# Macaron transformer layer on eight cores: the q/k/v projections of the next head group move into the query blocks of the current one

## The chip, the cores and the metric

The program runs on all eight cores of one Trainium2 chip. Each core computes one of the eight sequences of the batch, with no exchange between cores. The metric is the time of one execution on the slowest core, in microseconds (us). The cores' engines are TensorE (PE, matmuls), VectorE (DVE), ScalarE (ACT), GpSimd (POOL) and SyncE (SP); each works through its own list of instructions in order and waits on semaphores for the others.

## What is computed

The input is 2048 tokens of width 1024 per core. The layer is a mixture-of-experts feed-forward step, an attention step, and the same feed-forward step again, each on a layer-normed input and added to the running x. The change is in the attention alone:

```python
proj = x @ w_in                        # x: layer-normed [2048, 1024]
k, v, q = jnp.split(proj, 3, axis=-1)  # 16 heads of 64 each
scores = jnp.einsum('bhqd,bhkd->bhqk', q, k) * scale
scores = scores + _tisa_bias(amplitudes, sharpness, offsets, s)[None]
weights = jax.nn.softmax(scores, axis=-1)
attn = jnp.einsum('bhqk,bhkd->bhqd', weights, v)
gated = attn.transpose(0, 2, 1, 3).reshape(b, s, d) @ w_gate + b_gate
a, g = jnp.split(gated, 2, axis=-1)
return a * jax.nn.sigmoid(g)
```

The bias depends only on head and on the distance between query and key, so the kernel keeps exp(bias) as a table of 4095 values per head in DRAM (`etab_d`) and multiplies exp(scores) by it.

## The kernel before

Everything is written with explicit semaphores. `ph.op(engine, ...)` appends an instruction to one engine's list, `ph.wait(engine, event)` makes the next instruction of that list wait. So the order in which the Python loops run is the order of each engine.

`attn_phase` (from L723) works on `NGRP` = 8 groups of two heads. One group g of the loop has these parts:

- **flush_pending** finishes the last query block of the group before. `flush_a` (L816): TensorE turns the row of softmax sums with four small transposes (L824), VectorE takes the reciprocal (L832), GpSimd stores it to DRAM (`rbc_scr`) and, when the store has landed, reads it back spread over the partitions (`at_bca`). `flush_b` (L848): VectorE waits for that read and multiplies the block's result by it (L858 into `at_af` for the even head, L870 into `at_stag` for the odd one, from which GpSimd moves it on by DMA).
- **Projection** (L906): for k, v, q in turn and for four chunks of 512 tokens, a step of eight matmuls of 128x512 adds up into one half (`sl`) of the PSUM tile `p_pr` (`at_ppr`). The halves take turns, so a step runs while the other half is read out: to `kT` (L918) and `vT` (L925) by a ScalarE cast, to `qT` (L932) by VectorE. After the last step GpSimd loads the weights `w_in` of group g+2 into the buffer that has become free (`issue_win`, L763).
- **Softmax bound** (L948 to L1018): ScalarE issues four DMAs that copy `kT` and `qT` with their partition halves exchanged into `kM` and `qM`; it squares q and k (L960, L962); TensorE sums (L971), VectorE takes maxima (`reduce_max`, L979), and a chain of small steps over TensorE, VectorE and ScalarE ends in the exponent's offset `negmh` (L1018).
- **Query blocks**: for each of the two heads (`hl`), TensorE first transposes v (L1032), VectorE copies it (L1040); then four blocks `qg` of 512 queries follow. A block (hl,qg) has four rounds `q`. In a round TensorE computes scores of 512 keys in two halves of `p_s` (L1082, L1096), each when ScalarE has read the half's previous contents; ScalarE takes exp of each half (L1113, 128x1024); VectorE multiplies by the table (L1134, four of 128x512); TensorE multiplies by v (`emit_pv`, L1062) into the half `par` of `p_pr`, one round behind the scores. At the block's end ScalarE copies that half out (L1157, `at_attsb`). Blocks take the two halves of `p_pr` in turn; `pat_free[half]` is the event after which a half can be written again. `flush_a` of a block is written in round 1 of the next one, `flush_b` at the next one's end.
- **Table loads**: `issue_next_equad` (L788) loads the table of one head, 128 x 3968 values, into one of two buffers `ebuf`, on SyncE's queue for even and ScalarE's for odd loads, when the head two before is done; a block reads at offset `512 * qg`.

After the eight groups comes the gated output projection (L1206 on), which isn't changed but for a buffer.

Of the kernel before, what the change touches and what calls it, by code (L numbers as in the profile page):

```python
# [95 lines left out]
def build_nc(stop=None):  # L96
# [31 lines left out]
    with ExitStack() as octx:  # L128
# [17 lines left out]
        def tev():  # L146
            return ("t", cnt["t"])
# [575 lines left out]
        def attn_phase():  # L723
            with ExitStack() as ctx:
# [12 lines left out]
                ebuf = [SB(ctx, f"at_e{i}", [128, 3968], F16) for i in range(2)]  # L737
# [50 lines left out]
                def issue_next_equad():  # L788
# [4 lines left out]
                    h_ = EQ[i]  # L793
                    buf = i % 2
                    qu = EQUEUE[buf]
                    if e_free_ev[buf] is not None:
# [4 lines left out]
                        _ap(etab_d, h_ * TAB,  # L801
                            [(1, 128), (1, 3968)]), ESEM[buf])
# [88 lines left out]

                for g in range(NGRP):
# [3 lines left out]
                    ph.wait("tensor", pat_free[0])  # L896
                    ph.wait("tensor", pat_free[1])
                    ev_evac = [None, None]
                    for part in range(3):
                        for tch in range(4):  # L900
                            sl = tch % 2
                            if ev_evac[sl] is not None:
                                ph.wait("tensor", ev_evac[sl])
                            for c in range(NDCH):
                                ph.op("tensor", lambda h, part=part, tch=tch,
                                      c=c, wbuf=wbuf, sl=sl: h.matmul(  # L906
                                    p_pr[:, sl * 512: sl * 512 + 512],
                                    win[wbuf][:, part * 1024 + c * 128:
                                              part * 1024 + c * 128 + 128],
                                    hf[:, c * S + tch * 512:  # L910
                                       c * S + tch * 512 + 512],
                                    start=(c == 0), stop=(c == NDCH - 1)),
                                    inc="t" if c == NDCH - 1 else None)
                            ev_mm = tev()
                            if part == 0:
                                ph.wait("scalar", ev_mm)
                                ev_evac[sl] = ph.op(
                                    "scalar", lambda h, tch=tch, sl=sl: h.copy(  # L918
                                        out=kT[:, tch * 512: tch * 512 + 512],
                                        in_=p_pr[:, sl * 512: sl * 512 + 512]),  # L920
                                    inc="s")
                            elif part == 1:
                                ph.wait("scalar", ev_mm)
                                ev_evac[sl] = ph.op(
                                    "scalar", lambda h, tch=tch, sl=sl: h.copy(  # L925
                                        out=vT[:, tch * 512: tch * 512 + 512],
                                        in_=p_pr[:, sl * 512: sl * 512 + 512]),
                                    inc="s")
                            else:
                                ph.wait("vector", ev_mm)  # L930
                                ev_evac[sl] = ph.op(
                                    "vector", lambda h, tch=tch, sl=sl: h.tensor_scalar(  # L932
                                        out=_ap(qT, 2047 - tch * 512,
                                                [(S, 128), (-1, 512)]),
                                        in0=p_pr[:, sl * 512: sl * 512 + 512],
                                        scalar1=0.125, scalar2=None,
                                        op0=ALU.mult), inc="v")
                    ev_proj_s = sev()
                    ev_proj_v = vev()
                    pat_free[0] = ev_evac[0]  # L940
                    pat_free[1] = ev_evac[1]
                    win_free[wbuf] = tev()
                    if g + 2 < NGRP:
                        issue_win(g + 2)
# [3 lines left out]
                    for (dst, srct) in ((kM, kT), (qM, qT)):  # L948
# [391 lines left out]
```

How the kernel before makes its waits and increments, by code:

```python
                def run(h, items=items):  # L64
                    waited = {}
                    pending = {}
                    def flush():
                        for sname in sorted(pending):
                            v = pending[sname]
                            if waited.get(sname, -1) < v:
                                h.wait_ge(self.sems[sname], v)
                                waited[sname] = v
                        pending.clear()
                    for it in items:
                        if it[0] == "w":
                            sname, v = it[1]
                            if pending.get(sname, -1) < v:
                                pending[sname] = v
                        else:
                            flush()
                            _, fn, inc, amt = it
                            ins = fn(h)
                            if inc is not None:
                                ins.then_inc(self.sems[inc], amt)
                    flush()
```

## Time and profile before

| | us |
|---|---|
| median of 2 runs | 3674.85 (3673.9 to 3675.81) |
| profiled execution | 3672.66 |
| its span on the slowest core (core 4) | 3671.1 |
| spans of the eight cores | 3638.1 to 3671.1 |
| attention's head groups, from the first projection's weights to the last copy | 1328 to 2440 |

The page gives for core 4 of the span: TensorE 74% busy, VectorE 31%, ScalarE 26%, GpSimd 5%, and a mean granted TensorE clock of 0.881. The line of the granted clock reads 1.00 where TensorE runs at its full 2.4 GHz and 0.50 at 1.2 GHz; a value between is a mean over a stretch with both. In timeline rows the columns are: start in us from the span's start, duration in us, engine, line, operation, output<-inputs with shapes, how many instructions are merged, and in brackets how long the engine had been idle before and who released it. A merged row's duration runs from the first to the last of its instructions.

### The profile page before, as it was taken

The numbers are of one execution on the slowest core, as the hardware profiler recorded it, in microseconds if no ns is written. First come the engines' busy times: TensorE is split into PE (matmuls) and PEld (weight loads), VectorE is DVE, ScalarE is ACT, GpSimd is POOL, SyncE is SP. The second block draws the span as 40 slices with busy tenths as digits, with TensorE's granted clock in tenths as the row PEclk, the third lists the DMA queues.
The fourth block names the chain that finished last, engine by engine and source line by source line (L and its number), as shares of the span: only waits on it lengthen the run. The fifth ranks groups of instructions, "written<-read, shape, count | busy, mean of one in ns | idle before, by whom it ended". The sixth has DMA issues, their size and how long they took to land. (4 is left out here: it accounts for less than half of the span.)

```text
span 3671.1 us, 36071 instructions; the slowest of 8 cores (3638.1 to 3671.1 us)
## 1 busy us (share of the span) xinstructions
PE 2730.1 (74%) x12493; PEld 1176.3 (32%) x12680; DVE 1143.0 (31%) x2466; ACT 969.4 (26%) x993; POOL 173.6 (5%) x266
## 2 busy tenths in 40 slices
PE   0355577999999757667767677756629999999996
PEld 0122223444444322222222222213314444444443
DVE  2521101303122225445345345432252123031220
ACT  2300000101011047557557556541121011010110
POOL 0001110000000001010010000010000000000000
PEclk9677889999999868888788787879959999999998
DMA  4279976645454231221221222232108555454545
GB/s 117 25 125 163 171 170 183 192 141 173 145 172 155 92 60 31 43 42 24 38 53 23 39 44 21 31 24 23 12 1 197 149 161 177 141 186 138 174 153 177
DMA packets 200559, 384.26 MB, mean 105 GB/s; under 512 B 59152, under 2 KB 108560, under 8 KB 200224
## 3 DMA queue, kind: packets, MB, share of 16 engines
q1 hardware_dynamic: 92624, 304.44, 27.5%
q0 software_dynamic: 103008, 56.80, 13.2%
q10 hardware_dynamic: 4752, 20.71, 1.9%
q8 instruction: 106, 1.74, 0.2%
q14 instruction: 69, 0.57, 0.1%
HBM read 381.41 MB, written 40.37 MB: 115 GB/s over the span
## 5 line engine op out<-in xcount | busy, mean ns | idle before, releaser
L577 PE MATMUL f_p<-hf,f_wgu 128*128 128x512 bf16 x2508 | 602.8, 392 | 137.0 <-DMA f_wgu<-wu_r 91.0
L654 PE MATMUL f_p<-f_pall,f_wdb 128*128 128x512 bf16 x2506 | 568.3, 386 | 53.6 <-DMA f_wdb<-wd_r 33.8
L588 PE MATMUL f_p<-hf,f_wgu 128*128 128x512 bf16 x2508 | 574.6, 379 | 2.7
L1113 ACT ACTIVATE at_pexp<-at_ps,at_ngm 128x1024 bf16<-128x1024 f32 x512 | 531.7, 1112 | 104.1 <-PE at_ps L1082 90.6
L1134 DVE TENSOR_TENSOR at_pt<-at_pexp,at_e 128x512 bf16<-128x512 bf16 x1024 | 386.9, 421 | 288.1 <-ACT at_pexp L1113 259.5
L608 ACT ACTIVATE f_gs<-f_p 128x1024 bf16<-128x1024 f32 x160 | 163.7, 1023 | 1073.3 <-PE f_p L577 1073.3
L577 PEld LDWEIGHTS f_p<-hf,f_wgu 128*128 128x128 bf16 x2560 | 256.0, 101 | 459.6 <-issue 179.1
L1062 PE MATMUL at_ppr<-at_pt,at_vtm 128*65 128x512 bf16 x1024 | 344.6, 453 | 69.7 <-DVE at_pt L1134 69.6
L616 DVE TENSOR_TENSOR f_t<-f_p,f_bc 128x1024 f32<-128x1024 f32 x128 | 156.7, 1225 | 707.9 <-PE f_p L588 707.9
L654 PEld LDWEIGHTS f_p<-f_pall,f_wdb 128*128 128x128 bf16 x2560 | 252.9, 99 | 369.0 <-issue 80.4
L588 PEld LDWEIGHTS f_p<-hf,f_wgu 128*128 128x128 bf16 x2560 | 250.5, 98 | 302.0
L711 DVE TENSOR_TENSOR xt<-xt,f_p 128x128 f32<-128x128 f32 x256 | 53.5, 280 | 634.9 <-PE f_p L695 630.7
L686 ACT ACTIVATE f_stg<-f_p 128x1024 f32<-128x1024 f32 x32 | 31.0, 1021 | 651.3 <-PE f_p L654 640.9
L1082 PE MATMUL at_ps<-at_qT,at_kT 64*128 64x512 bf16 x256 | 116.4, 455 | 93.2 <-ACT at_pexp L1113 92.6
L906 PE MATMUL at_ppr<-hf,at_w 128*128 128x512 bf16 x752 | 172.3, 390 | 16.1 <-DMA at_w<-w_in 13.7
L1062 PEld LDWEIGHTS at_ppr<-at_pt,at_vtm 128*65 128x65 bf16 x1024 | 96.3, 124 | 268.1 <-issue 256.2
L1096 PE MATMUL at_ps<-at_qT,at_kT 64*128 64x512 bf16 x256 | 118.1, 461 | 57.0 <-ACT at_pexp L1113 56.9
L624 DVE TENSOR_TENSOR f_pall<-f_t,f_gs 128x1024 bf16<-128x1024 f32 x128 | 156.8, 1225 | 11.8
L1206 PE MATMUL at_ps<-at_af,at_w 128*128 128x512 bf16 x499 | 118.9, 391 | 23.0 <-DMA at_w<-w_gate 22.4
L336 PE MATMUL ln_ph<-identb_s,ln_ht 128*128 128x128 bf16 x384 | 48.5, 306 | 115.8 <-ACT ln_ht L327 113.0
L1096 PE MATMUL at_ps<-at_qM,at_kM 64*128 64x512 bf16 x256 | 119.8, 468 | 0.0
L1082 PE MATMUL at_ps<-at_qM,at_kM 64*128 64x512 bf16 x256 | 117.7, 460 | 0.0
(107 smaller groups left out, 1366.2 us busy)
## 6 DMA issues: line engine op xcount, KB each, us to landing
f_wgu<-wbf_scr SPq DMA_DIRECT2D x140, 1024.0 KB, 6.1
f_wdb<-wbf_scr SPq DMA_DIRECT2D x140, 512.0 KB, 3.6
f_bc<-comb_scr SPq DMA_DIRECT2D x128, 256.0 KB, 6.5
wbf_scr<-f_wgu SPq DMA_DIRECT2D x20, 1024.0 KB, 7.8
wbf_scr<-f_wdb SPq DMA_DIRECT2D x20, 512.0 KB, 4.7
f_wgu<-wg_r POOLq DMA_DIRECT2D x16, 512.0 KB, 17.1
f_wgu<-wu_r POOLq DMA_DIRECT2D x16, 512.0 KB, 23.7
f_wdb<-wd_r POOLq DMA_DIRECT2D x16, 512.0 KB, 7.2
```

The lines of the kernel that those rows point to most:

```text
L577: pg=pg, tb=tb: h.matmul(pg[:, mc * 512: mc * 512 + 512], wgu[buf][:, c * 256 + mc * 128: c * 256 + mc * 128 + 128], hf[:, c * S + tb * TB ...
L588: pu=pu, tb=tb: h.matmul(pu[:, mc * 512: mc * 512 + 512], wgu[buf][:, 2048 + c * 256 + mc * 128: 2048 + c * 256 + mc * 128 + 128], hf[:, c ...
L608: ev_sil = ph.op("scalar", lambda h, pg=pg, buf=buf: h.activation(out=gsil[:, buf * 1024: buf * 1024 + 1024], in_=pg[:, :], func=AF.Silu), ...
L616: ev_t1 = ph.op("vector", lambda h, pu=pu, buf=wbuf: h.tensor_tensor(out=t1[:, :].rearrange("p (a b) -> p a b", a=2), in0=pu[:, :].rearran ...
L624: ev_p = ph.op("vector", lambda h, u=u, buf=buf: h.tensor_tensor(out=p_all[:, u * 1024: u * 1024 + 1024], in0=t1[:, :], in1=gsil[:, buf * ...
L654: mc=mc, po=po, col=col, u=u: h.matmul(po[:, col: col + 512], wdb[buf][:, mc * 1024 + dch * 128: mc * 1024 + dch * 128 + 128], p_all[:, u ...
L906: c=c, wbuf=wbuf, sl=sl: h.matmul(p_pr[:, sl * 512: sl * 512 + 512], win[wbuf][:, part * 1024 + c * 128: part * 1024 + c * 128 + 128], hf[ ...
L1062: par=par: h.matmul(p_pr[0:65, par * 512: par * 512 + 512], vtm[:, c * 65: c * 65 + 65], pt[:, (q % 2) * 2048 + j * 512: (q % 2) * 2048 + ...
L1082: kk=kk, qq=qq, qg=qg: h.matmul(p_s[:, (c % 4) * 512: (c % 4) * 512 + 512], kk[bb: bb + 64, c * 128: c * 128 + 128], qq[bb: bb + 64, qg * ...
L1096: kk=kk, qq=qq, qg=qg: h.matmul(p_s[:, (c % 4) * 512: (c % 4) * 512 + 512], kk[bb: bb + 64, c * 128: c * 128 + 128], qq[bb: bb + 64, qg * ...
L1113: hh=h_: h.activation(out=pexp[:, (q % 2) * 2048 + half_i * 1024: (q % 2) * 2048 + half_i * 1024 + 1024], in_=p_s[:, half_i * 1024: half_i ...
L1134: ebuf_i=ebuf_i: h.tensor_tensor(out=pt[:, (q % 2) * 2048 + j * 512: (q % 2) * 2048 + j * 512 + 512], in0=pexp[:, (q % 2) * 2048 + j * 512 ...
```

## The change

The projection of group 0 stays in front. The projection of group g+1 is no longer a stage of its own: its twelve steps are emitted two at a time at the head of six of the eight query blocks of group g, ahead of the scores of the block. k takes steps 0 to 3, q 4 to 7, v 8 to 11. Both steps of a pair write the half `1 - par` of `p_pr`, the one that the block's PV doesn't use, each waiting for `pat_free` of that half. `kT` and `qT` are doubled. For space, the table buffers shrink to 128 x 2432 values and are loaded for every block (64 loads in place of 16), and `gsg` of the output projection shares `att_sb`. The weights of group g+2 are requested behind step 11 of group g+1.

```diff
-                kT = SB(ctx, "at_kT", [128, S], BF16)
+                kTs = [SB(ctx, f"at_kT{i}", [128, S], BF16) for i in range(2)]
-                qT = SB(ctx, "at_qT", [128, S], BF16)
+                qTs = [SB(ctx, f"at_qT{i}", [128, S], BF16) for i in range(2)]
-                ebuf = [SB(ctx, f"at_e{i}", [128, 3968], F16) for i in range(2)]
+                ebuf = [SB(ctx, f"at_e{i}", [128, 2432], F16) for i in range(2)]
-                gsg = SB(ctx, "at_gsg", [128, 2 * 512], F32)
+                gsg = None
...
+                gsg = att_sb
...
-                        EQ.append(_g * 2 + _hl)
+                        for _qg in range(4):
+                            EQ.append((_g * 2 + _hl, _qg))
...
-                        _ap(etab_d, h_ * TAB,
-                            [(1, 128), (1, 3968)]), ESEM[buf])
+                        _ap(etab_d, h_ * TAB + 512 * qg,
+                            [(1, 128), (1, 2432)]), ESEM[buf])
...
+                pj_ev = {}
+                PSTEPS = {(0, 0): (0, 1), (0, 1): (2, 3), (0, 2): (4, 5),
+                          (0, 3): (6, 7), (1, 0): (8, 9), (1, 1): (10, 11)}
+
+                def emit_proj_step(gn, idx, islot):
+                    part = (0, 2, 1)[idx // 4]
+                    tch = idx % 4
+                    nbuf = gn % 2
+                    if idx == 0:
+                        ph.waits("tensor", win_dma[gn])
+                    ph.wait("tensor", pat_free[islot])
+                    for c in range(NDCH):
+                        ph.op("tensor", lambda h, part=part, tch=tch, c=c,
+                              nbuf=nbuf, islot=islot: h.matmul(
+                            p_pr[:, islot * 512: islot * 512 + 512],
...
+                            inc="t" if c == NDCH - 1 else None)
+                    ev_mm = tev()
+                    if part == 0:
+                        ph.wait("scalar", ev_mm)
+                        ev = ph.op("scalar", lambda h, tch=tch, islot=islot,
+                                   nbuf=nbuf: h.copy(
...
+                    elif part == 1:
+                        ph.wait("scalar", ev_mm)
...
+                    else:
+                        ph.wait("vector", ev_mm)
+                        ev = ph.op("vector", lambda h, tch=tch, islot=islot,
+                                   nbuf=nbuf: h.tensor_scalar(
...
+                    pat_free[islot] = ev
+                    if idx == 7:
+                        pj_ev[("v", gn)] = vev()
+                    if idx == 11:
+                        pj_ev[("s", gn)] = sev()
+                        win_free[nbuf] = tev()
+                        if gn + 2 < NGRP:
+                            issue_win(gn + 2)
+
+                for idx0 in range(12):
+                    emit_proj_step(0, idx0, idx0 % 2)
+
                 for g in range(NGRP):
-                    wbuf = g % 2
                     flush_pending()
-                    ph.waits("tensor", win_dma[g])
...
-                    if g + 2 < NGRP:
-                        issue_win(g + 2)
+                    kTb, qTb = kTs[g % 2], qTs[g % 2]
+                    ev_proj_s = pj_ev[("s", g)]
+                    ev_proj_v = pj_ev[("v", g)]
...
                             par = hgi % 2
+                            if g + 1 < NGRP:
+                                for idx in PSTEPS.get((hl, qg), ()):
+                                    emit_proj_step(g + 1, idx, 1 - par)
...
-                                eoff = 512 * qg
+                                eoff = 0
...
-                                if q == 3 and qg == 3:
+                                if q == 3:
                                     eq_use[0] = ei + 1
                                     e_free_ev[ei % 2] = mult_ev[q % 2][1]
                                     issue_next_equad()
```

## Rows read from the trace of the kernel before

**Rows 1.** Stages: from:to, length, busy PE, PEld, DVE, ACT, POOL, clock, DMA share, GB/s.

```profile
1466.70:1489.20 22.50, 21.22 (x98) 9.88 (x100) 3.63 (x6) 4.72 (x9) 2.26 (x5) 1.00 0.17 52
1508.30:1604.10 95.80, 69.00 (x296) 22.35 (x296) 54.25 (x143) 69.82 (x71) 8.72 (x16) 0.85 0.12 23
```

**Rows 2.** Timeline, the end of a query block and the start of the next.

```profile
1568.16 0.59 PE L1062 MATMUL at_ppr<-at_pt,at_vtm 128*65 128x512 bf16 x2 [0.34 <-DVE at_pt L1134]
1568.68 0.39 PE L1082 MATMUL at_ps<-at_qT,at_kT 64*128 64x512 bf16 x1
...
1568.84 0.58 ACT L1157 COPY at_attsb<-at_ppr 65x512 f32<-65x512 f32 x1 [1.69 <-PE at_ppr L1062]
...
1569.33 2.11 ACT L1113 ACTIVATE at_pexp<-at_ps,at_ngm 128x1024 bf16<-128x1024 f32 x2
```

**Rows 3.** Timeline, the end of group 0 and the projection of group 1.

```profile
1465.41 0.32 ACTq L51 DMA_DIRECT2D at_e<-etab_scr  x1
...
1466.16 0.58 ACT L1157 COPY at_attsb<-at_ppr 65x512 f32<-65x512 f32 x1 [1.69 <-PE at_ppr L1062]
...
1466.89 0.60 PE L824 MATMUL at_pbc<-idf_s,at_attsb 1*128 1x1 f32 x4 [0.82 <-ACT at_attsb L1157]
...
1467.60 0.18 DVE L832 RECIPROCAL at_rrec<-at_pbc 128x4 f32<-128x4 f32 x1 [1.67 <-PE at_pbc L824]
...
1469.42 0.58 ACT L918 CAST at_kT<-at_ppr 128x512 bf16<-128x512 f32 x1 [2.67 <-PE at_ppr L906]
1471.14 0.58 ACT L918 CAST at_kT<-at_ppr 128x512 bf16<-128x512 f32 x1 [1.14 <-PE at_ppr L906]
...
1489.20 1.12 ACTq L51 DMA_DIRECT2D at_kM<-at_kT  x2
```

**Rows 4.** Timeline, the first cast of two later projections.

```profile
1748.44 0.58 ACT L918 CAST at_kT<-at_ppr 128x512 bf16<-128x512 f32 x1 [4.36 <-PE at_ppr L906]
...
2308.49 0.58 ACT L918 CAST at_kT<-at_ppr 128x512 bf16<-128x512 f32 x1 [4.11 <-PE at_ppr L906]
```

**Rows 5.** Stages within the query blocks of group 1 (the clock: third column from last).

```profile
1504.00:1516.00 12.00, 8.49 (x40) 3.15 (x42) 4.75 (x13) 7.78 (x9) 0.00 (x0) 0.50 0.01 2
...
1524.00:1530.00 6.00, 6.00 (x20) 1.72 (x20) 3.06 (x9) 3.46 (x4) 1.12 (x2) 0.52 0.14 15
...
1540.00:1560.00 20.00, 13.20 (x78) 4.61 (x76) 12.50 (x32) 15.78 (x17) 1.60 (x3) 1.00 0.26 65
```

**Rows 6.** Timeline, VectorE after a group's end and in the bound.

```profile
1474.91 0.68 DVE L870 TENSOR_TENSOR at_stag<-at_attsb,at_bca 64x512 bf16<-64x512 f32 x1 [7.13 <-DMA at_bca<-rbc_scr]
...
1496.42 3.67 DVE L979 TENSOR_REDUCE at_mt<-at_ps 2x1 f32<-2x512 f32 x6 [7.30 <-PE at_ps L971]
...
2315.26 0.68 DVE L870 TENSOR_TENSOR at_stag<-at_attsb,at_bca 64x512 bf16<-64x512 f32 x1 [8.81 <-DMA at_bca<-rbc_scr]
```

**Rows 7.** DMA issues of the head groups: count, KB each, median us to landing.

```profile
at_e<-etab_scr SPq DMA_DIRECT2D x7, 992.0 KB, 4.7
...
at_w<-w_in POOLq DMA_DIRECT2D x21, 256.0 KB, 8.7
...
at_qM<-at_qT ACTq DMA_DIRECT2D x16, 256.0 KB, 8.4
```

**Rows 8.** Timeline, the last query block of a head and the start of the next.

```profile
1545.41 0.58 ACT L1157 COPY at_attsb<-at_ppr 65x512 f32<-65x512 f32 x1 [1.69 <-PE at_ppr L1062]
...
1549.94 0.55 POOL L51 DMA_DIRECT2D rbc_scr<-at_rrec  x1 [9.26 <-DVE at_pt L1134]
...
1552.59 0.53 POOL L51 DMA_DIRECT2D at_bca<-rbc_scr  x1 [2.10 <-DMA rbc_scr<-at_rrec]
...
1555.98 0.68 DVE L858 TENSOR_TENSOR at_af<-at_attsb,at_bca 64x512 bf16<-64x512 f32 x1 [0.42 <-DMA at_bca<-rbc_scr]
1556.38 0.58 ACT L1157 COPY at_attsb<-at_ppr 65x512 f32<-65x512 f32 x1 [1.69 <-PE at_ppr L1062]
...
1558.45 0.76 DVE L1134 TENSOR_TENSOR at_pt<-at_pexp,at_e 128x512 bf16<-128x512 bf16 x2 [0.79 <-ACT at_pexp L1113]
```

More of the change, by code:

```diff
@@ L890, in attn_phase @@
                 att_ev = [None, None]
+                pj_ev = {}
[12 more added lines that the diff above has]
+                            p_pr[:, islot * 512: islot * 512 + 512],
+                            win[nbuf][:, part * 1024 + c * 128:
+                                      part * 1024 + c * 128 + 128],
+                            hf[:, c * S + tch * 512:
+                               c * S + tch * 512 + 512],
+                            start=(c == 0), stop=(c == NDCH - 1)),
+                            inc="t" if c == NDCH - 1 else None)
[4 more added lines that the diff above has]
+                                   nbuf=nbuf: h.copy(
+                            out=kTs[nbuf][:, tch * 512: tch * 512 + 512],
+                            in_=p_pr[:, islot * 512: islot * 512 + 512]),
+                            inc="s")
+                    elif part == 1:
+                        ph.wait("scalar", ev_mm)
+                        if ev_vtmfree is not None:
+                            ph.wait("scalar", ev_vtmfree)
+                        ev = ph.op("scalar", lambda h, tch=tch, islot=islot:
+                                   h.copy(
+                            out=vT[:, tch * 512: tch * 512 + 512],
+                            in_=p_pr[:, islot * 512: islot * 512 + 512]),
+                            inc="s")
+                    else:
+                        ph.wait("vector", ev_mm)
+                        ev = ph.op("vector", lambda h, tch=tch, islot=islot,
+                                   nbuf=nbuf: h.tensor_scalar(
+                            out=_ap(qTs[nbuf], 2047 - tch * 512,
+                                    [(S, 128), (-1, 512)]),
+                            in0=p_pr[:, islot * 512: islot * 512 + 512],
+                            scalar1=0.125, scalar2=None,
+                            op0=ALU.mult), inc="v")
+                    pat_free[islot] = ev
[6 more added lines that the diff above has]
+                            issue_win(gn + 2)
@@ L892, in attn_phase @@
+                for idx0 in range(12):
+                    emit_proj_step(0, idx0, idx0 % 2)
                 for g in range(NGRP):
-                    wbuf = g % 2
                     flush_pending()
-                    ph.waits("tensor", win_dma[g])
[L896 to L937, printed above, removed]
@@ L947, in attn_phase @@
                     ph.wait("scalar", ev_proj_v)
-                    for (dst, srct) in ((kM, kT), (qM, qT)):
+                    for (dst, srct) in ((kM, kTb), (qM, qTb)):
                         for bnd in range(2):
@@ L1077, in attn_phase @@
                                     c = q * 4 + j
-                                    kk = kT if j % 2 == 0 else kM
-                                    qq = qT if j % 2 == 0 else qM
+                                    kk = kTb if j % 2 == 0 else kM
+                                    qq = qTb if j % 2 == 0 else qM
                                     bb = base if j % 2 == 0 else mbase
@@ L1091, in attn_phase @@
                                     c = q * 4 + j
-                                    kk = kT if j % 2 == 0 else kM
-                                    qq = qT if j % 2 == 0 else qM
+                                    kk = kTb if j % 2 == 0 else kM
+                                    qq = qTb if j % 2 == 0 else qM
                                     bb = base if j % 2 == 0 else mbase
```

16 lines of the change are left out of this document (6 added, 10 removed).

## The prediction

> **What bounds the kernel now.** I read the page first, then cut the attention phase into stages, then read single boundaries in the timeline. All rows are of core 4, the slowest, in the one profiled execution (span 3671.1 us, run 3672.7 us; the median of the runs, 3674.85 us, is 3.75 us above that span). On the page no engine is full over the whole span, but the change touches the attention phase alone, so its stages decide. A group of two heads has three. In the projection TensorE is full, with clock 1.00 [rows 1]. In the softmax bound, from 1489.20 on, nearly everything waits in a chain. In the eight query blocks TensorE shows 69.0 and ScalarE 69.8 of 95.8 us [rows 1]: neither is full. Those blocks are a loop of hand-overs: scores, exp, multiply, PV, with each engine in its own order. The reader should look at the end of a block [rows 2]: TensorE issues the last PV matmuls (1568.16), then the scores of the next block (1568.68); ScalarE, which has stood for 1.69 us, copies the PV result out (1568.84) and starts the next exp at 1569.33. At a block's end TensorE's instruction order *is* the path: ScalarE has nothing to do until the next scores are there.
>
> **What is removed.** From the copy that ends a group (1466.16) to the mirror transfers that open the bound (1489.20) are 23.04 us [rows 3]. What remains of it is the copy and the four transposes of flush_a, over when VectorE's reciprocal follows at 1467.60 [rows 3]: 1.5 us. Saved: 21.5 us at each of the seven boundaries between groups (the first projection stays in front), 150.5 us. Three of the seven projections started at the lower clock: ScalarE waited 4.36 to 4.11 us for the first cast (first and last of the three in [rows 4]) where the usual wait is 2.67 [rows 3], 4.6 us more in sum. Saved in all: 155 us.
>
> **What is added at a block boundary.** The twelve steps of the next group now go in pairs at the head of six blocks: (0,0) to (0,3), (1,0), (1,1). They stand in TensorE's order between the last PV of the old block and the first scores of the new one, the very place that [rows 2] show to be the path. Both steps of a pair use the half of p_pr that the new block doesn't use, and that is the half the old block has just filled. So step 1 waits for the copy of the old block, and step 2 waits for the cast of step 1. The rows give: the copy ends at 1466.74 and TensorE answers at 1466.89, 0.15 us later; taking that and the 0.60 us of transposes off the 2.68 us to the cast at 1469.42 leaves 1.93 us from a step's first matmul to its cast; a cast takes 0.58; steps that overlap their casts follow each other in 1.72 us [rows 3]. From the end of the old copy (1569.42, [rows 2]) to the new scores: 0.15 + 1.93 + 0.58 + 0.15 + 1.72 = 4.53 us, so 1573.95 where 1568.68 stood: 5.3 us. The second cast lies beside the new scores: exp would start 0.49 us after it, and now starts 0.65 us after the scores, so it costs 0; alone it would be 0.58. For the query steps a VectorE instruction takes the cast's place; the difference is left out. Nothing else lies beside the steps, for ScalarE and VectorE have finished the old block and need the scores for the new. Five such boundaries: 26.4 us a group.
>
> The first block, (0,0), has its half free for long and needs no copy: 1.93 + 0.58 + 0.15 + 1.72 = 4.4 us at full clock. But TensorE comes out of the bound at clock 0.50 and stays there for 12 us [rows 5], and a step at that level takes up to 4.36 - 2.67 = 1.7 us more [rows 3, 4]: up to 7.8 us. I take 6.0, since some of the clock should come back during the steps. Sum: 7 x (26.4 + 6.0) = 227 us against 155 saved, **+72 us**. In short, matmuls are moved from a place where they ran without a stop to one where they stop twice in each pair, and still nothing runs beside them.
>
> **What is late next.** (a) At a group's end flush_b waits in VectorE's queue for the broadcast reciprocal, and its multiply runs from 1474.91 to 1475.59 [rows 6]. Today the projection covers that. Without it the bound's first reduce_max would be due 1.5 + 7.22 = 8.7 us after the copy began (1489.20 to 1496.42, [rows 3, 6]), but it is behind the multiply in the same queue. That ends 9.4 us after the copy began, and 12.1 us in the slowest group (2315.94, with the copy over at 2308.49 - 4.11 = 2304.38; [rows 4, 6]). The mirror transfers (8.4 us to landing for at_qM, [rows 7]) would now be in flight with the reciprocal as well. The eight reductions run one behind the other, so a late first one is a late bound. Bounds 0.7 and 6 us, taken 3.0, near the slowest row: 7 x 3 = **+21 us**.
>
> (b) The load of w_in for the group after next is issued behind step 11, at the head of block (1,1), on GpSimd's queue: three transfers of 256 KB, 8.7 us to landing [rows 7]. In a block whose scores start at 1545.25 (0.16 us before the copy, as in [rows 2]) the reciprocal's store is issued 4.7 us later (1549.94), its return 2.65 us after that, and VectorE wants it 10.7 us after the scores (1555.98) [rows 8]. If the store sits behind the weights it lands some 11 us after the scores (2.7 us of issues and 8.7), the return some 15; the multiply that now starts at 1558.45, 13.2 us after the scores [rows 8], starts near 15.4. That is 2.2 us in each of five groups, **+11 us**; 0 if the small transfer slips through, 30 if the whole wait shows. No row shows a small transfer behind weights. The Trainium skill (DMA: Bandwidth & Descriptors, Queues, rings and completion order) says that a DMA engine consumes one ring's descriptors in order, by which the store would sit behind; without the page the bounds stay as they are.
>
> (c) The bias table is now read in 64 pieces of 608 KB, not 16 of 992 KB. A 992 KB piece lands in 4.7 us [rows 7]; a smaller one has a whole block, at least 10.97 us [rows 8], before it is used: 0. Without that cover it would be up to 64 x 4.7 us. Every second one is issued from ScalarE, 0.32 us at 1465.41, inside the 1.69 us in which it waits for PV anyway [rows 3]: 0. In front of the mirror transfers such a piece may hold up their issue; 0 taken, up to 3 us a group at the high end. The second kT and qT, and gsg in att_sb's place, cost no instruction.
>
> Sum: 72 + 21 + 11 = +104 us: span 3775 us, and on the median 3674.85 + 104 = **3779 us**.
>
> **Rivals.**
> *The clock pays it back* (a little slower, within 2%). Within blocks the clock falls to 0.52 and comes back to 1.00 [rows 5]. The eight blocks of this group take 95.8 / 8 = 11.98 us on average [rows 1]; one without a fall takes 10.97, from copy to copy [rows 8]. More matmuls inside the blocks could keep the clock up: 42 blocks x 1.0 us give back 42 us, 3737 us. For it: TensorE stands still for less of the time. Against it: the two new waits of each pair are new gaps, and the unbroken 22 us at clock 1.00 are gone. The Trainium skill (TensorE: Matmul & The Clock Gate, Part 1) calls the lower clock the default, which activity lifts and idling brings back; by that rule this rival is open, and the trace agrees as far as the clock is 1.00 in the dense projection and 0.50 after the bound.
> *The moved steps run at the lower clock* (slower still). Three of seven projections began so [rows 4]. Half of the 70 steps that stand behind a copy, at 1.69 us more, are +59 us: 3838 us. Against it: the score matmuls at the block ends last 0.39 us [rows 2], as they do at clock 1.00, and the other boundaries between blocks read alike.
> *The projection hides after all* (faster). If ScalarE's and VectorE's work covered the steps wholly, only (a) and (b) would be left: 3675 - 155 + 32 = 3552 us. To be faster by 2% a pair must cost under (155 - 73 - 32) / 42 = 1.2 us. Its sixteen matmuls alone take 3.44 us at full clock; only scores that overtake them could do it, and [rows 2] show scores strictly behind PV.
>
> **How the numbers follow.** A measurement of this kernel can tell about 2%, 73.5 us, from no change: 3601 to 3748. Forecast 0.60, clock pays back 0.26, lower clock 0.09, hidden 0.05. Of the forecast all lies above 3748 but for a corner where (a) and (b) are at their low ends and part of the clock comes back (72 + 5 + 0 is only just over 2%), one tenth of it, which goes to the middle: slower 0.54 + 0.09 = 0.63, same 0.26 + 0.06 = 0.32, faster 0.05. The range is 3725 (clock repaid, low ends) to 3830 (high ends of (a) and (b), or some slow steps); it leaves out the hidden case and the outer parts of the other two.
>
> **What would show it.** The stage between a group's last copy and the mirrors shrinks from 23 to about 1.5 us (else the removal fails). In blocks with steps the scores start some 5.3 us later behind PV, with a TensorE wait on the copy and one on the cast, and the block takes near 17 us; periods near 12 would refute the argument and mean faster. The first reduce_max stands behind the multiply of at_stag. Block (1,2) shows a wait on at_bca of some 4 us. A granted clock well above 0.85 in the blocks, which is today's [rows 1], would speak for the first rival. Most of all I would be wrong if TensorE got through a pair in far less than 5 us.

## The result: 3.6% slower, and the profile after

The changed kernel takes 3812 us (median) where the kernel before takes 3675: a ratio of 1.0356, 95% interval 1.0329 to 1.0384, or +131 us by the ratio. The forecast was slower, 3779 us, range 3725 to 3830. In some executions the cores of one die run at a lower granted clock and take longer; every ratio here is of executions without that, and the profile of the spread version below is read on core 0, whose die didn't have it.

The profiled execution took 3828 us, the longest of ten (3782 to 3828). Its slowest core is core 6, span 3826.9 us; the eight cores now lie between 3749.9 and 3826.9, wider apart than before. TensorE's busy time grew by 26 us in the section below and that of ScalarE and VectorE not at all: what grew is waiting. First the section of the eight head groups, from the first mirror transfer to the last copy, in the columns of [rows 1]; before:

```profile
1352.30:2440.00 1087.70, 764.41 (x3302) 266.78 (x3316) 507.66 (x1297) 648.28 (x679) 100.73 (x174) 0.83 0.21 35
```

and after:

```profile
1362.20:2602.70 1240.50, 790.47 (x3316) 262.90 (x3316) 506.45 (x1297) 648.20 (x679) 100.61 (x174) 0.82 0.33 51
```

153 us more, almost the same work, and more transfers in flight. The granted clock is the same as a mean over the section, but not by stages. Group 1's eight query blocks and the bound behind them (group 2's), after, in the same columns:

```profile
1535.40:1673.20 137.80, 94.40 (x412) 31.82 (x412) 56.77 (x147) 76.03 (x82) 11.41 (x19) 0.88 0.33 46
1674.50:1697.90 23.40, 4.91 (x11) 1.25 (x11) 6.99 (x16) 5.21 (x5) 2.16 (x4) 0.50 0.36 76
```

In the blocks the clock is 0.88 where [rows 1] had 0.85, and over the five blocks (0,1) to (1,1) of seven groups it is 0.91 against 0.85. In the bound it is lower, 0.52 against 0.61 in the mean of the seven behind a boundary, and the projection stage, which ran at 1.00 in [rows 1], is gone. Next a block boundary of the changed kernel in the timeline, the one between (0,1) and (0,2) of group 0, which answers to [rows 2]:

```profile
1417.47 0.59 PE L1079 MATMUL at_ppr<-at_pt,at_vtm 128*65 128x512 bf16 x2 [0.34 <-DVE at_pt L1151]
...
1418.15 0.58 ACT L1174 COPY at_attsb<-at_ppr 65x512 f32<-65x512 f32 x1 [1.69 <-PE at_ppr L1079]
1418.88 1.89 PE L907 MATMUL at_ppr<-hf,at_w 128*128 128x512 bf16 x8 [0.82 <-ACT at_attsb L1174]
1420.88 0.69 DVE L935 TENSOR_SCALAR at_qT<-at_ppr 128x512 bf16<-128x512 f32 x1 [2.35 <-PE at_ppr L907]
1421.71 1.89 PE L907 MATMUL at_ppr<-hf,at_w 128*128 128x512 bf16 x8 [0.95 <-DVE at_qT L935]
1423.53 0.39 PE L1099 MATMUL at_ps<-at_qT,at_kT 64*128 64x512 bf16 x1
```

The reader should see the two brackets on TensorE: 0.82 us for the copy of the old block, 0.95 us for the step's own readout. The scores start 5.38 us after the copy; in [rows 2] they start 0.16 us before it. With a ScalarE cast in the middle the figure is 5.25, 5.41 us later than before. On the slowest core of either profile the parts of a group come out so (measured between copy starts, mirror issues and the offset's copy at L1018, after: L1032; means of seven: the blocks of groups 0 to 6, the bounds of groups 1 to 7, which stand behind a boundary):

| part of a group | before | after | difference | x 7 | predicted |
|---|---|---|---|---|---|
| last copy to mirror issue | 23.9 | 1.42 | -22.5 | -158 | -155 |
| bound, mirror issue to offset | 15.5 | 22.8 | +7.3 | +51 | +21 |
| block (0,0) | 14.5 | 21.4 | +6.9 | +48 | +42 |
| five blocks (0,1) to (1,1) | 61.3 | 88.6 | +27.4 | +192 | +185 |
| block (1,2) | 12.3 | 14.4 | +2.0 | +14 | +11 |
| block (1,3) | 11.8 | 12.2 | +0.4 | +3 | 0 |

The differences sum to 150 us; the other 3 of the section lie in group 0's bound and the last group's blocks. Now a group's end (group 1's), which answers to [rows 3] and [rows 6]:

```profile
1672.36 0.33 ACTq L51 DMA_DIRECT2D at_e<-etab_scr  x1
...
1673.11 0.58 ACT L1174 COPY at_attsb<-at_ppr 65x512 f32<-65x512 f32 x1 [1.69 <-PE at_ppr L1079]
...
1674.53 1.13 ACTq L51 DMA_DIRECT2D at_kM<-at_kT  x2
...
1677.13 0.57 POOL L51 DMA_DIRECT2D rbc_scr<-at_rrec  x1
...
1683.07 0.53 POOL L51 DMA_DIRECT2D at_bca<-rbc_scr  x1 [5.37 <-DMA rbc_scr<-at_rrec]
1688.55 0.68 DVE L872 TENSOR_TENSOR at_stag<-at_attsb,at_bca 64x512 bf16<-64x512 f32 x1 [12.41 <-DMA at_bca<-rbc_scr]
1689.16 4.86 DVE L993 TENSOR_REDUCE at_mt<-at_ps 2x1 f32<-2x512 f32 x8
1689.98 2.38 PE L985 MATMUL at_ps<-at_pt,ind_s 128*2 128x512 bf16 x4 [8.69 <-DVE at_mt L993]
```

The mirrors start 1.42 us after the copy, as forecast. But VectorE stands for 12.41 us on the broadcast reciprocal, and the eight reductions start the moment its multiply is done, 14.6 us after the mirrors where [rows 3, 6] had 7.2. TensorE stands for 8.69 us on them. Last, the transfers of this part of the kernel (count, KB each, median us to landing), which answer to [rows 7]:

```profile
at_e<-etab_scr SPq DMA_DIRECT2D x31, 608.0 KB, 5.6
...
at_bca<-rbc_scr POOLq DMA_DIRECT2D x62, 128.0 KB, 5.7
...
rbc_scr<-at_rrec POOLq DMA_DIRECT2D x62, 2.0 KB, 3.0
```

In the kernel before the read of at_bca lands in 3.6 us and the small store in 1.7.

### The profile page after: what moved, and what is told of

It reads as the page before. It is cut to its first block and busy times, and to the rows that moved or that the text cites. A ratio compares the mean times of both kernels' runs of the same rounds, so it can differ in the third digit from the quotient of the medians.

```text
span 3826.9 us, 36228 instructions; the slowest of 8 cores (3749.9 to 3826.9 us)
## 1 busy us (share of the span) xinstructions
PE 2766.2 (72%) x12680; PEld 1172.5 (31%) x12680; DVE 1141.6 (30%) x2466; ACT 969.5 (25%) x993; POOL 173.5 (5%) x266
## 5 line engine op out<-in xcount | busy, mean ns | idle before, releaser
L907 PE MATMUL at_ppr<-hf,at_w 128*128 128x512 bf16 x768 | 206.0, 419 | 89.8 <-ACT at_attsb L1174 24.6
L1099 PE MATMUL at_ps<-at_qT,at_kT 64*128 64x512 bf16 x256 | 111.7, 436 | 96.0 <-ACT at_pexp L1130 95.7
L624 DVE TENSOR_TENSOR f_pall<-f_t,f_gs 128x1024 bf16<-128x1024 f32 x128 | 156.8, 1225 | 11.8
L1113 PE MATMUL at_ps<-at_qT,at_kT 64*128 64x512 bf16 x256 | 113.6, 444 | 63.8 <-ACT at_pexp L1130 63.7
L907 PEld LDWEIGHTS at_ppr<-hf,at_w 128*128 128x128 bf16 x768 | 74.2, 104 | 213.5 <-issue 153.9
L1113 PE MATMUL at_ps<-at_qM,at_kM 64*128 64x512 bf16 x256 | 115.3, 451 | 0.0
```

The costliest lines, as they stand in the source:

```text
L624: ev_p = ph.op("vector", lambda h, u=u, buf=buf: h.tensor_tensor(out=p_all[:, u * 1024: u * 1024 + 1024], in0=t1[:, :], in1=gsil[:, buf * ...
L907: nbuf=nbuf, islot=islot: h.matmul(p_pr[:, islot * 512: islot * 512 + 512], win[nbuf][:, part * 1024 + c * 128: part * 1024 + c * 128 + 12 ...
L1113: kk=kk, qq=qq, qg=qg: h.matmul(p_s[:, (c % 4) * 512: (c % 4) * 512 + 512], kk[bb: bb + 64, c * 128: c * 128 + 128], qq[bb: bb + 64, qg * ...
```

## The experiments

The theory: the pair of steps stands in TensorE's order on the path and costs two stops and sixteen matmuls (5.3 us); then flush_b's multiply makes the bound late, and the weights make block (1,2) late. The rivals: the clock decides; the transfers decide; the stops cost nothing by themselves. Differences in us are those of the ratios to the kernel before, times 3675; by the intervals of the two ratios, the distance of a run from the changed kernel is known to within 13 to 33 us. Where block lengths are given for a run, they are of its slowest core unless said otherwise.

### One half for each step of a pair

```diff
-                                    emit_proj_step(g + 1, idx, 1 - par)
+                                    emit_proj_step(g + 1, idx,
+                                                   par if idx % 2 == 0 else 1 - par)
```

> The changed kernel with one edit: the first step of a pair writes the half par of p_pr (free since the copy of two blocks ago), the second the half 1 - par, so that neither step waits for the other's cast and the first doesn't wait for the old block's copy. Theory (the pair stands in TensorE's order between PV and scores, and costs two stops plus sixteen matmuls): scores start 3.3 us after the copy begins instead of 5.25 (0.52 + 3.44 us of matmuls after the last PV), 1.9 us less at 35 boundaries and 0.9 less at 7 first blocks: -73 us against the changed kernel, some +60 us against the kernel before. Rival (the pair is paid for by the lower clock and by waits on transfers, the stops are covered by something else): less than 25 us gained.

Measured: ratio 1.0123 (1.0038 to 1.0208), 86 us less than the changed kernel (known to within 33); 73 were expected. The timeline of a boundary:

```profile
1402.97 0.59 PE L1080 MATMUL at_ppr<-at_pt,at_vtm 128*65 128x512 bf16 x2 [0.35 <-DVE at_pt L1152]
1403.40 3.62 PE L907 MATMUL at_ppr<-hf,at_w 128*128 128x512 bf16 x16
...
1403.65 0.58 ACT L1175 COPY at_attsb<-at_ppr 65x512 f32<-65x512 f32 x1 [1.69 <-PE at_ppr L1080]
...
1406.95 0.39 PE L1100 MATMUL at_ps<-at_qT,at_kT 64*128 64x512 bf16 x1
```

Sixteen matmuls in one piece, right behind PV, and the scores 3.30 us after the copy: the two stops are gone, the matmuls still show in full. The stops had been worth more than 1.9 us on average, for the mean from copy to scores fell from 5.76 to 3.43 us: with the waits on the reciprocal below, the second stop was often longer than 0.95.

### One matmul for each step

```diff
-                    for c in range(NDCH):
+                    last = NDCH - 1 if gn == 0 else 0
+                    for c in range(last + 1):
...
```

> The changed kernel with one matmul in each moved projection step instead of eight (the sums over the other seven chunks of the model width are left out for groups 1 to 7), all waits, casts and positions kept. Theory (a pair costs two stops of some 1.9 us in sum and sixteen matmuls of 3.44 us, all shown): fourteen matmuls fewer take 14 x 0.215 = 3.0 us off each pair; scores start 2.2 us after the copy instead of 5.25; 42 pairs x 3.0 = -126 us against the changed kernel, about 3686 us. Rival (the stops are what costs, the matmuls run beside them): under 1 us per pair, less than 50 us gained. What stays against the kernel before is then the stops and the late transfers alone.

Measured: ratio 1.004 (0.9984 to 1.0096), 116 us less; 126 were expected. The boundary, now with 2.57 us from copy to scores:

```profile
1418.18 0.58 ACT L1175 COPY at_attsb<-at_ppr 65x512 f32<-65x512 f32 x1 [1.69 <-PE at_ppr L1080]
1418.91 0.38 PE L908 MATMUL at_ppr<-hf,at_w 128*128 128x512 bf16 x1 [0.82 <-ACT at_attsb L1175]
1419.39 0.69 DVE L936 TENSOR_SCALAR at_qT<-at_ppr 128x512 bf16<-128x512 f32 x1 [1.36 <-PE at_ppr L908]
1420.23 0.58 PE L908 MATMUL at_ppr<-hf,at_w 128*128 128x512 bf16 x1 [0.95 <-DVE at_qT L936]
1420.75 0.60 PE L1100 MATMUL at_ps<-at_qT,at_kT 64*128 64x512 bf16 x1
```

Both stops are there to the hundredth (0.82 and 0.95), and fourteen matmuls less are 2.8 us less, so stops and matmuls add up and nothing runs beside either. Here the clock speaks too: scores last 0.60 us, and over the section the granted clock is 0.73, against 0.82 in the changed kernel. With seven eighths of the moved matmuls gone TensorE falls to 1.2 GHz more often, and the five blocks came down by 2.4 us each (17.7 to 15.4), less than the 3.3 us by which the mean from copy to scores fell; they are still 3.1 us longer than in the kernel before (12.3), the lower clock included.

### flush_b behind the bound

```diff
                 for g in range(NGRP):
-                    flush_pending()
+                    flush_a()
...
                     expAB[0] = None
+                    flush_b()
```

> The changed kernel with one edit: flush_b of a group's last block is written behind the softmax bound (after negmh) instead of ahead of it. Theory (the first reduce_max stands in VectorE's queue behind the multiply that waits for the broadcast reciprocal): mirror issue to first reduce_max falls from 12 to 17.7 us to the 7.2 us of the kernel before, the bound from 22.75 to some 15.5 us on the slowest core, 7 us at each of 7 groups: -25 us (a core whose bound takes 19.3) to -50 us (one at 22.75) against the changed kernel. Rival (the table piece and the mirror transfers make the squares or the sums late): the bound stays above 20 us and the gain is under 10 us.

Measured: ratio 1.0246 (1.0204 to 1.0287), 40 us less. The bound fell from 22.8 to 14.6 us, below the 15.5 of the kernel before. A group's end:

```profile
1519.86 1.13 ACTq L51 DMA_DIRECT2D at_kM<-at_kT  x2
...
1525.11 0.53 POOL L51 DMA_DIRECT2D at_bca<-rbc_scr  x1 [3.93 <-DMA rbc_scr<-at_rrec]
1525.56 4.87 DVE L993 TENSOR_REDUCE at_mt<-at_ps 2x1 f32<-2x512 f32 x8 [5.50 <-PE at_ps L985]
1533.51 0.68 DVE L872 TENSOR_TENSOR at_stag<-at_attsb,at_bca 64x512 bf16<-64x512 f32 x1
```

The reductions wait for TensorE's sums again, 5.7 us after the mirrors, and the multiply finds its data there. The squares and sums were never late; the rival falls. That it is 5.7 and not 7.2 is new: the mirror transfers are issued faster than when the weights' load was issued with them (the two issues of at_qM took 3.28 us at 1490.35 in the kernel before, 1.63 us at 1675.69 in the changed one), as they already were in the kernel before for the last two groups, which request no weights (the two issues 1.7 us, the reductions 5.6 to 5.7 us after the mirrors).

### The weights requested behind the bound

```diff
-                        if gn + 2 < NGRP:
-                            issue_win(gn + 2)
+                        if gn == 0:
+                            issue_win(2)
...
                     expAB[0] = None
+                    if g > 0 and g + 2 < NGRP:
+                        issue_win(g + 2)
```

> The changed kernel with one edit: the load of w_in for group g+2 is requested behind the softmax bound of group g, not behind step 11 in block (1,1). Theory (the reciprocal's small transfers of block (1,1) sit behind the weights and make block (1,2) late): block (1,2) falls from 14.4 us (mean of the first seven groups) to 12.3, some -13 us against the changed kernel, near the limit of what can be measured; the cost may come back in block (0,0) or (0,1) if the weights are still in flight there. Rival (block (1,2) is late for another reason, such as the table piece): it stays at 14 or more.

Measured: ratio 1.0328 (1.0289 to 1.0368), 10 us less, which the intervals don't tell from none. The profile does tell: block (1,2) came down from 14.4 to 12.1 us in the mean of seven. These are single cores, and in the changed kernel this mean differs from core to core (11.8 to 14.5 us); with the late request it is 11.8 to 12.5 on all eight. In the changed kernel the chain can be read in block (1,1) of group 0 (core 6):

```profile
1473.80 2.65 POOL L51 DMA_DIRECT2D at_w<-w_in  x3 [7.14 <-PE at_ps L1113]
...
1478.12 0.58 POOL L51 DMA_DIRECT2D rbc_scr<-at_rrec  x1 [1.67 <-DVE at_pt L1151]
...
1483.28 0.54 POOL L51 DMA_DIRECT2D at_bca<-rbc_scr  x1 [4.58 <-DMA rbc_scr<-at_rrec]
...
1488.87 0.68 DVE L872 TENSOR_TENSOR at_stag<-at_attsb,at_bca 64x512 bf16<-64x512 f32 x1 [3.27 <-DMA at_bca<-rbc_scr]
```

The 2 KB store, whose landing lets the read be issued, holds it back 4.58 us behind the weights, and block (1,2)'s first multiplies stand behind L872. At this place the read is issued 5.2 to 8.0 us after the store in the five groups that request weights and 2.2 to 3.5 us in the other three; with the request moved it is 2.2 to 2.8 us in all but the last group (4.6). In the kernel before it was mostly 2.2.

### The table loads alone

The kernel before with only the table's edits of the diff.

> The kernel before with only the change of the table loads: 64 pieces of 608 KB in buffers of 2432 values, the projection left as a stage of its own. Theory (the pieces cost nothing by themselves): 3675 us, within 0.5% of the kernel before, blocks at 12.2 us. Rival (the pieces slow the small transfers of the reciprocal, which land in 5.7 us in the changed kernel where 3.6 stood, and that alone lengthens the blocks): 10 to 40 us slower than before, with VectorE waits on at_bca.

Measured: ratio 1.0032 (1.0005 to 1.0059), +12 us. Neither side was quite right: the pieces seem to cost something, at the lowest end of what the rival gave, and the interval all but reaches none. Their transfers:

```profile
at_e<-etab_scr SPq DMA_DIRECT2D x31, 608.0 KB, 4.6
...
at_bca<-rbc_scr POOLq DMA_DIRECT2D x60, 128.0 KB, 5.5
```

at_bca lands in 5.5 us instead of 3.6; the store, in 1.8, doesn't suffer. On core 6, the slowest, the blocks' means rise by 0.2 to 0.7 us in six of the eight positions, but that core also has the lowest granted clock (0.875 over the span; the others 0.881 to 0.888), and over the eight cores the mean block is 12.52 us against 12.46. So the 12 us belong to the slowest core, and how much of them is the pieces' doing isn't shown.

### The changed kernel without table traffic

```diff
                     i = eq_ptr[0]
+                    if 2 <= i < len(EQ):
+                        e_dma_ev[i] = e_dma_ev[i - 2]
+                        eq_ptr[0] = i + 1
+                        return
```

> The changed kernel with the table loaded only for the first two blocks; all later loads are left out and the blocks multiply by what lies in the buffers. Theory (the table pieces lengthen the reciprocal's read from 3.6 to 5 us and hold up the mirror transfers, so that the multiply of flush_b is later in blocks and at a group's end): landing of at_bca back to about 3.6 us, the bound from 22.5 to 17 to 19 us, blocks shorter by 0.3 to 0.5 us: 35 to 50 us off the changed kernel. Rival (the pieces matter only for the 12 us that they cost in the kernel before): 10 to 15 us off, the bound stays above 21 us because of the mirror transfers.

Measured: ratio 1.0318 (1.0272 to 1.0365), 14 us less, known to within 20: the rival's figure for the time, and not told from none, while 35 to 50 us lie outside that. at_bca lands in 3.7 us again, so its lateness is the table pieces' doing; the store still takes 2.7 us, against 1.7 in the kernel before, so its lateness isn't. The bound only fell to 19.9 us; over the cores it is 18.2 to 20.1, against 18.8 to 23.3 in the changed kernel, which neither side had quite. What keeps it there isn't the table; the mirrors, in flight at the same time, are what is left, but they were not taken away in a run. The five blocks didn't get shorter (88.3 us a group against 88.6). My expectation, 35 to 50 us, was wrong.

### All three edits together

> The changed kernel with the three edits together: two halves for a pair, flush_b behind the bound, weights requested behind the bound. Theory (the three costs stand one behind the other on the path and add up): -86, -40 and -10 us against the changed kernel, to about 1.0356 - 0.0233 - 0.0110 - 0.0028 = 0.9985 of the kernel before, 3670 us: with every stop gone, the bare matmuls at the head of the blocks cost what the removed stage saved. Rival (they cover each other): above 1.01.

Measured: ratio 0.9935 (0.9911 to 0.9959), 155 us less than the changed kernel; the three alone sum to 136. They add up, and the 19 us between are inside the intervals. All of the loss is undone, and the version is 24 us faster than the kernel before, though sixteen matmuls still stand bare at each boundary (mostly 3.29 us from copy to scores, as in the first experiment). On the slowest core the eight blocks of a group are 20.9 us longer than before (5.6 of it in (0,0), 14.4 in the next five), while the removed stage gives 22.5 and the bound, at 14.7, another 0.8; the clock over the section is 0.84.

### The steps spread over the rounds

A step is no longer one piece. In all eight blocks of a group two of its matmuls stand between the two halves of a round's scores, and for the even head two more ahead of PV; VectorE reads the step out ahead of the multiplies of rounds 1 and 3 (odd head: 3). Its core:

```diff
                                 ev_sA = tev()
+                                ev_chm = None
+                                if q in ch:
+                                    ix, c0, cm, c1 = ch[q]
+                                    emit_chunk(g + 1, ix, 1 - par, c0, cm)
...
                                 ev_sB = tev()
+                                if q in ch and c1 > cm:
+                                    emit_chunk(g + 1, ix, 1 - par, cm, c1)
...
+                                if ev_chm is not None:
+                                    emit_cast(g + 1, ix, 1 - par, ev_chm)
```

> A version in which the projection does run beside ScalarE: the steps are cut into chunks of two matmuls, put between the two halves of the scores of a round (four a round for the even head, two of them ahead of PV; two a round for the odd head), in all eight blocks; the casts are VectorE's, ahead of the multiplies of rounds 1 and 3; flush_b and the weights' request stand behind the bound. Theory (what costs is the place in TensorE's order): TensorE stands still for 0.6 to 1.3 us in each round, two matmuls take 0.43 us; the blocks lengthen by 1 to 2 us instead of 5.4; 155 us saved less 56 x 1.5 us and 12 us for the table pieces: 3675 - 155 + 84 + 12 = 3616 us, 0.98 of the kernel before (range 0.965 to 1.0). Rival (TensorE is full in the blocks when the clock is low, and every matmul put there shows): above 1.0.

Measured: ratio 0.9538 (0.9466 to 0.961, from two executions), 170 us faster than the kernel before, more than the range allowed. Read on core 0: the bound 14.7 us; block (0,0), behind the bound, 15.0; the even head's other blocks 12.8 us with two steps each; the odd head's mostly 11.5 with one (23 of 28; the rest are 12.1 to 17.0, and the mean is 11.9). In the kernel before the positions behind (0,0) take 12.2 on average. The mis-sized term is the blocks': 84 us were allowed for them, and the eight blocks of a group take 101.2 us against 99.97, 8 us over seven groups. An odd-head boundary and the first round behind it:

```profile
2154.33 0.39 PE L1157 MATMUL at_ps<-at_qT,at_kT 64*128 64x512 bf16 x1
...
2154.49 0.58 ACT L1244 COPY at_attsb<-at_ppr 65x512 f32<-65x512 f32 x1 [1.69 <-PE at_ppr L1137]
2154.97 4.38 ACT L1198 ACTIVATE at_pexp<-at_ps,at_ngm 128x1024 bf16<-128x1024 f32 x4
2155.10 0.68 DVE L872 TENSOR_TENSOR at_stag<-at_attsb,at_bca 64x512 bf16<-64x512 f32 x1 [1.44 <-DMA at_bca<-rbc_scr]
2155.21 0.59 PE L963 MATMUL at_ppr<-hf,at_w 128*128 128x512 bf16 x2 [0.49 <-ACT at_attsb L1244]
2155.74 0.39 PE L1177 MATMUL at_ps<-at_qT,at_kT 64*128 64x512 bf16 x1
```

Scores come 0.16 us ahead of the copy, as in [rows 2], and the projection's two matmuls (L963) run while ScalarE is in its exps. Why odd-head blocks with more matmuls are shorter than blocks without them, the stages tell: four odd-head blocks with a step each (group 6), and the seven later blocks of group 7, which carry none:

```profile
2131.60:2177.30 45.70, 38.83 (x192) 13.12 (x188) 30.12 (x77) 35.80 (x36) 5.44 (x10) 1.00 0.37 70
2208.50:2293.40 84.90, 61.16 (x268) 20.07 (x264) 48.03 (x127) 61.58 (x64) 8.70 (x16) 0.86 0.29 58
```

At clock 1.00 a block takes 45.7 / 4 = 11.4 us with a step in it, at 0.86 it takes 84.9 / 7 = 12.1 us without one. Same run, same code around them. What a step costs when the clock stays up is the difference to a block at 1.00 without one, 10.98 us (the last section has the rows): 0.5 us, and 1.8 us for the two steps of an even-head block.

### The spread alone

The same placement, with flush_b and the weights' request where the changed kernel has them.

> The version with the steps spread over the rounds, but with flush_b ahead of the bound and the weights requested right behind step 11, as in the changed kernel: what the placement and VectorE's casts do alone. Theory (placement is the main cost, the late multiply at a group's end a second one that adds to it): blocks as in the spread version (12.8 and 11.5 us), the bound back at 19 to 23 us; 35 to 55 us slower than the spread version, 0.964 to 0.972 of the kernel before, against 0.9538 with all three. Rival (flush_b's position is what gave most of the gain): above 0.99.

Measured: ratio 0.975 (0.9729 to 0.9771), 78 us slower than the spread version with the late flush_b and the late weights, and 223 us faster than the changed kernel. All but one of the blocks with steps behind (0,0) are 12.8 or 11.4 to 11.5 us, and the bound is back at 23.9. Expected were 35 to 55 us of difference; the bound alone gives 7 x 9.2 = 64 us. The placement, with the readouts' move to VectorE, is the larger part all the same.

## Why the prediction was right, and which terms were off

- **Place on the path.** Right. [rows 2] showed scores behind PV and ScalarE with nothing to do; the brackets after show the rest. The first two experiments take the term apart: stops 1.8 to 2.3 us, matmuls 2.8 to 3.4 us, both shown in full. Predicted 5.3 us a boundary, measured 5.41 on an undisturbed one, 5.5 per block in the mean. At 192 us it is the largest of all, and that it was right kept the sum in its range.
- **Removal.** Right, 158 for 155 us. The stage shrank to 1.42 us against 1.5. The prediction counted three projections that started at the lower clock; the trace has four (first casts behind waits of 4.36, 4.15, 4.24 and 4.11 us), 6.2 us more in sum where 4.6 were taken, which gives 157.
- **First block.** 6.9 us against 6.0, inside its bounds of 4.4 and 7.8: after the bound the clock is at 1.2 GHz, as [rows 5] said, and the steps pay for it.
- **(a) The late multiply.** The mechanism was right and the size wrong: 3.0 us taken, bounds 0.7 to 6, measured 7.3 on core 6, outside the bounds, and 3.9 on core 2 of the same execution (bound 19.3 us there). The multiply was taken to end at worst 12.1 us after the copy, as in the slowest group before; at 1688.55 it ends 16.1 us after it. The read was issued 5.9 us after the store (1677.13 to 1683.07), where that took 2.2 to 4.3 us in the kernel before, and took 5.5 us itself, with the mirrors and a table piece in flight. Taking the multiply out of the way gave 40 us (to within 18), twice the +21, for it also brought the bound 0.9 us below that of the kernel before.
- **(b) The weights.** 2.8 us in the five groups that have the request (block (1,2) at 15.1 us on core 6), against 2.2. The 10 us by the ratios are no clear difference by themselves; that the cost is there is read from the block and from the store. The Trainium skill (DMA: Bandwidth & Descriptors, Queues, rings and completion order) says that descriptors are consumed in ring order, in a paragraph on the queues of SyncE and ScalarE; if GpSimd's queue goes by it too, the store begins behind the weights. The trace agrees, with 4.58 us at 1483.28 and the wait gone when the weights were moved.
- **(c) The table pieces at nothing.** Wrong by some 12 us (2 to 22). I priced their own deadline, which they meet, and not what they do to the small read next to them, 3.6 to 5.5 us. In the changed kernel this read stands ahead of VectorE's readout of the query steps: at 1437.16 the multiply runs, at 1437.77 the readout behind it, and TensorE's second stop is 1.45 us instead of 0.95. Such longer stops aren't the pieces' doing alone: without table traffic the mean from copy to scores is still 5.64 us, against 5.76.

```profile
1437.16 0.68 DVE L860 TENSOR_TENSOR at_af<-at_attsb,at_bca 64x512 bf16<-64x512 f32 x1 [3.46 <-DMA at_bca<-rbc_scr]
1437.77 0.68 DVE L935 TENSOR_SCALAR at_qT<-at_ppr 128x512 bf16<-128x512 f32 x1
1438.59 1.89 PE L907 MATMUL at_ppr<-hf,at_w 128*128 128x512 bf16 x8 [1.45 <-DVE at_qT L935]
```

On the slowest core of the two profiles the terms sum to 150 us where 104 were forecast, and 30 of the 46 missing are (a). The ratio gives 131, for the profiled execution is the longest of those that it is taken from.

**The clock rival** fell here by its price, though the sign named for it came in part: in the blocks with steps the clock did rise, from 0.85 to 0.91. It paid nothing back. Without a fall such a block takes from 16.4 us where 10.98 stood, 5.4 more; in the mean of the five positions it is 5.5 more; and what the blocks gained in clock the bound and the removed stage took (0.82 over the section against 0.83 before). The Trainium skill's rule (TensorE: Matmul & The Clock Gate, Part 1), that activity lifts the clock and idling brings it back, is borne out by the experiments on both sides: 0.73 over the section with one matmul a step, 0.86 in the spread version's blocks without steps and 1.00 in those of its blocks with a chunk in every round that are shown. My reading is that the change lacked not matmuls in the blocks but matmuls in the gaps. The rival in which the steps run at the lower clock fell as well, but for the first block: from the old block's copy to the new scores the clock is 1.00 at 30 of the 35 boundaries and 0.75 to 0.82 at five, where the rival had half of them at 0.50; at the head of (0,0) it is 0.50 to 0.71. That the projection can hide was right as a possibility and wrong for this order: scores had to come ahead of the steps.

**Open.** Why the bound is longer on some cores than on others of one execution (22.3 to 23.3 us on cores 0, 1, 6 and 7, 18.8 to 20.5 on the rest) wasn't pursued; what the mirrors do to the store and the read at a group's end wasn't taken apart; and how much of the spread version's gain beyond the forecast is the clock and how much the readouts' move to VectorE wasn't taken apart.

## What to carry to other kernels

Work meant to fill an engine's gaps must stand, in that engine's own order, behind the instruction that feeds the others, and in pieces no longer than the gap; put ahead of it, it is on the path, and every wait it brings is too. When a long stage is taken away, list what was waiting under its cover, above all small transfers with a round trip: each is due at its full landing time, in the company of whatever now starts with it. A large transfer that meets its own deadline can still have a price if a small one with a waiting engine shares the way.

## What the runs showed of the hardware

- A block's length goes with the granted clock: three blocks of the kernel before that follow each other on core 4, with the same work, take 10.98, 12.08 and 13.08 us at 1.00, 0.86 and 0.74. Over the blocks of all eight cores the means at these three levels are 10.98, 12.1 and 13.1 us. In the columns of [rows 1]:

```profile
1381.43:1392.41 10.98, 7.52 (x38) 2.56 (x36) 6.19 (x17) 8.72 (x9) 1.12 (x2) 1.00 0.10 13
1392.41:1404.49 12.08, 8.79 (x38) 2.73 (x36) 7.56 (x19) 8.83 (x9) 1.08 (x2) 0.86 0.11 11
1404.49:1417.57 13.08, 9.79 (x41) 3.06 (x38) 6.70 (x18) 8.85 (x9) 1.08 (x2) 0.74 0.07 11
```

- Blocks with more matmuls can be shorter: 11.4 us with a step of eight matmuls in each of four blocks and clock 1.00, against 12.1 us without them at 0.86, in one run. There eight matmuls a block cost less (0.5 us) than the falls of the clock that the blocks without them have.
- A 128 KB broadcast read goes from 3.6 to 5.5 us to landing when pieces of 608 KB are loaded once per block, though these add only some 12 us to the whole, and comes back to 3.7 without them. A 2 KB store takes 1.8 us beside the same pieces, 1.7 without them.
- A wait of TensorE on another engine's readout costs the same 0.82 us (ScalarE) and 0.95 us (VectorE) whether eight matmuls or one stand ahead of it.
